# Cross attention: another order of scores, maxima and weighings on TensorE, and later batches' queries moved behind the lead

## The chip, the cores and the metric

One core of one Trainium2 chip runs the whole program. The metric is the device time of one execution in microseconds. Of the kernel before there are three timed runs.

## The reference, cut to what matters

The reference is a small Perceiver-like network: x has 4 batches of 256 tokens with 256 channels, and each of two layers has a cross attention to a context of 4 x 4096 tokens, a self attention and a feed-forward part. The change touches only the cross attention, which is stage 0 and stage 3 of six stages:

```
q = layernorm(x) @ Wq (+ bq);  k = ctx @ Wk (+ bk);  v = ctx @ Wv (+ bv)     # 16 heads of 16 channels
x = x + (softmax(q k^T / 4) v) @ Wo (+ bo)                                  # 256 queries, 4096 keys per batch
```

## The kernel before, in words

Class `Cross` holds one cross-attention stage. Each engine's method (`pe`, `act`, `dve`, `pool`, `sp`) walks the same list of steps, `self.plan`, and issues its own part of each step, so the order of the list in `steps` is the order of the instructions on every engine, SyncE's queue of DMAs among them.

The keys of a batch are worked in 4 blocks of 1024, so there are 16 items (batch, block). An item has 4 groups of 4 heads, and such a group is called a quad here: 64 quads in a stage. A quad has 8 slots, one for each 128 keys of its block. For each slot there are a `scores` step (L891, 4 matmuls of 256 columns on 50 rows in each half of the array, followed by ScalarE's exponential, L683, into one of `NE = 4` buffers) and a `weigh` step (L921, the exponentials times the values, accumulated in one PSUM bank, on 128 rows and 17 columns). Ahead of it, `LEAD = 18` slots early, there is a `max` step (L907, 2 matmuls of 512 columns on 48 rows, followed by VectorE's reduction, L759), which finds each query's maximum over the block. `scores` and `max` share three PSUM units in turn; a unit is free again once ScalarE or VectorE has read it (`before`). ScalarE may write the exponentials of slot n only once slot n - 4 has been weighed.

Other steps lie between these. After the eighth maximum of a quad `place_max` combines the maxima on VectorE (L770; for the last block of a batch also L774 and L780, whose result ScalarE exponentiates, L712) and splits them on GpSimd. `max_rows` turns them on TensorE (L936), and SyncE writes them into spare rows of the queries with 4 DMAs (L576), for which the first `scores` of the next quad waits (`m_in`). `gather` turns the sums of a finished quad (L929). `combine` has three parts on VectorE (L791, L794, and L800 on), in four quads for each batch. `turn_out` and `project_out` finish a batch.

The jobs are projections of the context: `key` (L863, 6 matmuls of 512 columns) and `value` (L877, 12 of 256), 4 of each for an item, and `query` (L853), two for a batch. Keys and queries are copied by ScalarE, split into two parts by GpSimd (L606, L608; the two buffers alternate, and `kp_out` makes GpSimd wait until the write of the last but one has landed), written to DRAM by SyncE (L538) and read back in another layout: a batch's queries by `stack_q` (12 DMAs, L548), after waiting until both writes have landed, and half an item's keys by `stack_k` (6 DMAs, L479). One `stack_k` is issued in each even quad.

In the order before, two slots make a pattern: score, maximum, two weighings, score, maximum, and then one side step, which is `max_rows` with `gather` at the beginning of a quad, and otherwise a job if one may run. Values of an item may run only after its buffer is free (`may_fill`), so that the 8 jobs of an item fall into the first three quads of four, and the fourth has none. The 18 maxima of the lead run ahead of any score, with two side steps after each pair of them; the queries of batches 1 to 3 are among these.

Of the kernel before, what the change touches and what calls it, by code (L numbers as in the profile page):

```python
# [14 lines left out]
B, S, D = 4, 256, 256  # L15
# [231 lines left out]
class Cross(Stage):  # L247
# [25 lines left out]
    LEAD = 18  # L273
# [67 lines left out]
    def filling(self):  # L341


        values = lambda i: [("value", i, t) for t in range(self.KT // 2)]
        queries = lambda b: [("query", b, mt) for mt in range(2)]
        first = values(0)
        out = self.keys(0, 1) + first[0:2] + queries(1) + first[2:4] + queries(2) + queries(3)
        for i in range(1, self.ITEMS):
            out += self.keys(i, 0) + self.keys(i, 1) + values(i)
        return out  # L350

    def steps(self):
# [5 lines left out]
        else:  # L358
# [4 lines left out]
        total = self.SLOTS * self.ITEMS  # L363
        batch = self.SLOTS * self.NKB
        jobs = self.filling()
        outputs = [(batch * (b + 1) + at, (kind, b)) for b in range(B)
                   for at, kind in ((18, "turn_out"), (22, "project_out"))]
        for t in range(-self.LEAD, total + 24, 2):
            top = t + self.LEAD
            quad, at = divmod(t, 8)  # L370
            side = []
            if at == 0 and 0 <= quad + 1 < 4 * self.ITEMS:
                side.append(("max_rows", quad + 1))
            if at == 0 and 0 <= quad - 2 < 4 * self.ITEMS:
                side.append(("gather", quad - 2))
            if not side and outputs and outputs[0][0] <= t:
                side.append(outputs.pop(0)[1])
            while len(side) < (2 if t < 0 else 1) and jobs and self.may_fill(jobs[0], t):
                side.append(jobs.pop(0))
            for odd in range(2):  # L380
                if 0 <= t + odd < total:
                    out.append(("scores", t + odd))
                if top < total:
                    out.append(("max", top + odd))
                if odd == 0:
                    out += [("weigh", n) for n in (t - 2, t - 1) if 0 <= n < total]
            if top < total and top % 8 == 6:
                out.append(("place_max", top // 8))
            for step in side:
                out.append(step)  # L390
# [702 lines left out]
class Conv(Stage):  # L1093
# [3 lines left out]
    G = H // GH  # L1097
# [2042 lines left out]
```

## Time and profile before

| | us |
|---|---|
| median of three runs | 4365.25 (4364.61 to 4373.9) |
| span of the profiled execution | 4357.8 |
| TensorE, matmuls, busy | 3998.4 (92% of the span) |
| VectorE busy | 3011.4 (69%) |
| ScalarE busy | 2806.9 (64%) |
| GpSimd busy | 1811.5 (42%) |

The profile gives no whole time of its own execution beside the span; the median of the runs is 7.45 us above the span. The first cross attention lies from 0 to about 985 us, the second from about 2908 to 3885 us. In the digits of the page (40 slices, busy share in tenths) TensorE is at 9 in nearly every slice of both stages:

```profile
PE   4999999988979999999999999967999999976998
DVE  4777777767777767767677676644787877767745
PEclk7999999999989999999999999988999999988999
```

### The profile page before, as it was taken

What the parts mean: (1) busy time and instruction counts of PE and PEld (TensorE: products, weight loads), DVE (VectorE), ACT (ScalarE), POOL (GpSimd) and SP (SyncE); (2) the same over time, 40 slices, a digit from 0 to 9 for tenths busy, and PEclk for the clock granted to TensorE, in tenths of its full rate; (3) what the DMA queues carried; (4) which work ended last, traced back from release to release, by engine and by line L of the source; (5) the groups of instructions that cost most, each with busy time, mean ns of one, the idle gap of its engine ahead of it and who ended that gap; (6) DMA issues with size and microseconds to landing.
All of it is one profiled execution on the core that took longest, in us unless ns stands there. A gap on an engine that the chain in (4) does not pass through costs nothing. (4 is left out here: it accounts for less than half of the span.)

```text
span 4357.8 us, 81373 instructions
## 1 busy us (share of the span) xinstructions
PE 3998.4 (92%) x30320; PEld 2853.4 (65%) x30320; DVE 3011.4 (69%) x6897; ACT 2806.9 (64%) x5769; POOL 1811.5 (42%) x1862
## 2 busy tenths in 40 slices
PE   4999999988979999999999999967999999976998
PEld 3555555545757787887888888854555555535777
DVE  4777777767777767767677676644787877767745
ACT  2777777677967767777676776723676767654322
POOL 3333333204556555555556555523322322202644
PEclk7999999999989999999999999988999999988999
DMA  6666665536020110010100101027666666512265
GB/s 167 119 118 118 115 110 114 103 50 217 1 78 5 35 35 28 25 37 26 37 25 25 37 25 39 13 54 154 115 114 113 115 113 112 99 27 72 85 191 186
DMA packets 208194, 354.02 MB, mean 81 GB/s; under 512 B 26927, under 2 KB 110564, under 8 KB 205745
## 3 DMA queue, kind: packets, MB, share of 16 engines
q1 hardware_dynamic: 200217, 338.42, 35.4%
q0 software_dynamic: 7584, 10.39, 0.7%
q8 instruction: 243, 3.98, 0.4%
q14 instruction: 150, 1.23, 0.1%
HBM read 257.48 MB, written 114.98 MB: 85 GB/s over the span
## 5 line engine op out<-in xcount | busy, mean ns | idle before, releaser
L759 DVE TENSOR_REDUCE xa_m_part<-xa_unit 128x2 f32<-128x1024 f32 x1024 | 1247.7, 1224 | 515.3 <-PE xa_unit L907 513.8
L683 ACT ACTIVATE xa_ex<-xa_unit 128x1024 f32<-128x1024 f32 x1024 | 1029.8, 1019 | 259.7 <-PE xa_unit L891 254.4
L921 PE MATMUL xa_pv<-xa_ex,xa_vs 128*17 128x256 f32 x8192 | 546.5, 383 | 7.1 <-ACT xa_ex L683 7.0
L907 PE MATMUL xa_unit<-xa_ks,xa_q_base 48*128 48x512 f32 x2048 | 437.9, 425 | 117.8 <-ACT xa_ex L683 85.8
L1068 POOL TENSOR_SCALAR lt_p<-lt_p,lt_stat 128x192 f32<-128x192 f32 x384 | 355.3, 926 | 453.6 <-DVE lt_stat L1058 453.0
L891 PEld LDWEIGHTS xa_unit<-xa_q_base,xa_ks 50*128 50x128 f32 x4096 | 312.1, 185 | 316.2 <-issue 242.5
L891 PE MATMUL xa_unit<-xa_q_base,xa_ks 50*128 50x256 f32 x4096 | 502.5, 324 | 10.2 <-DVE xa_m_part L759 6.1
L1911 PE MATMUL lt_bank<-lt_wp,lt_xt 128*128 128x512 f32 x1728 | 465.1, 411 | 14.3 <-DVE lt_wp L1748 6.3
L1078 ACT ACTIVATE lt_p<-lt_p,lt_stat 128x128 f32<-128x128 f32 (+1 forms) x768 | 321.7, 420 | 157.2 <-DVE lt_stat L1053 154.5
L1911 PEld LDWEIGHTS lt_bank<-lt_wp,lt_xt 128*128 128x128 f32 x1728 | 314.5, 192 | 78.8 <-DVE lt_xt L1741 9.1
L618 POOL TENSOR_SCALAR xa_m_neg<-xa_m_blk 128x8 f32<-128x8 f32 x128 | 29.9, 233 | 780.4 <-DVE xa_m_blk L770 780.4
L1625 POOL TENSOR_TENSOR lt_r_qk<-lt_r_qk,lt_t_rot 128x512 f32<-128x512 f32 x192 | 268.0, 1397 | 202.5 <-DVE lt_t_rot L1779 196.8
L1053 DVE CUSTOM_DVE_ANT_0 lt_p<-lt_bank,lt_mask,lt_rq 128x128 f32<-128x128 f32 (+1 forms) x768 | 261.3, 377 | 122.2 <-PE lt_bank L1017 119.2
L921 PEld LDWEIGHTS xa_pv<-xa_ex,xa_vs 128*17 128x17 f32 x8192 | 186.4, 96 | 238.9 <-issue 123.5
L907 PEld LDWEIGHTS xa_unit<-xa_ks,xa_q_base 48*128 48x128 f32 x2048 | 193.1, 186 | 170.0 <-ACT xa_ex L683 117.1
L1632 POOL TENSOR_TENSOR lt_nrm<-lt_nrm,minus_half 128x16 f32<-128x16 f32 x96 | 282.0, 2937 | 22.4 <-DVE lt_nrm L1796 19.7
L1998 PE MATMUL lt_bank<-lt_ft,lt_w 128*128 128x256 f32 x1152 | 267.4, 382 | 9.4 <-DVE lt_ft L1856 5.9
L1686 ACT ACTIVATE lt_t_sq<-lt_bank 128x512 f32<-128x512 f32 x192 | 114.9, 598 | 226.1 <-DVE lt_t_rot L1779 226.1
L1998 PEld LDWEIGHTS lt_bank<-lt_ft,lt_w 128*128 128x128 f32 x1152 | 214.5, 191 | 41.5 <-issue 12.7
L606 POOL CAST xa_kp<-xa_k 128x512 fp32r<-128x512 f32 (+1 forms) x144 | 86.4, 600 | 341.1 <-ACT xa_k L663 138.9
L863 PE MATMUL xa_side<-xa_cxp,xa_wp 128*128 128x512 f32 x720 | 203.4, 419 | 10.6 <-DVE xa_cxp L742 10.6
L877 PE MATMUL xa_side<-xa_wp,xa_cxp 128*128 128x256 f32 x1488 | 208.4, 290 | 0.0
(334 smaller groups left out, 7903.3 us busy)
## 6 DMA issues: line engine op xcount, KB each, us to landing
xa_ks<-keys SPq DMA_DIRECT2D x372, 256.0 KB
keys<-xa_kp SPq DMA_DIRECT2D x128, 512.0 KB, 3.3
xa_cx<-in_ctx_t SPq DMA_DIRECT2D x64, 512.0 KB
lt_u<-in_lt_wqkv SPq DMA_DIRECT2D x54, 256.0 KB
places<-in_moe_blank SPq DMA_DIRECT2D x47, 258.0 KB, 8.6
moe_xs<-places SPq DMA_DIRECT2D x47, 258.0 KB
lt_w<-in_lt_w SPq DMA_DIRECT2D x6, 1536.0 KB
xa_q_base<-xa_m_rows SPq DMA_DIRECT2D x512, 2.0 KB
```

Of the source, the lines that this page charges most:

```text
L683: act.activation(x.ex[:, n % x.NE, :, :], x.place_of[step][:, :, :].rearrange("p o (j s) -> p (o j) s", j=2), ACT.Exp).then_inc(*x.ex_done ...
L759: dve.tensor_reduce(x.m_part[:, i % 2, qt, 2 * pair:2 * pair + 2, ch:ch + 1], x.place_of[step][:, :, :], AX.X, ALU.max).then_inc(*x.dve_ou ...
L891: mm = pe.matmul(bank[:, odd, pair * S:pair * S + S], x.ks[unit % x.NU][rows, 2 * (g % 2) + pair, kt * P:(kt + 1) * P], x.q_base[rows, 2 * ...
L907: mm = pe.matmul(bank[:, odd, :], x.q_base[rows, pair, b * S + qt * P:b * S + (qt + 1) * P], x.ks[unit % x.NU][rows, pair % 4, ch * 512:(c ...
L921: mm = pe.matmul(x.pv[32 * j:32 * j + x.VW, 0:S], x.vs[:, i % x.NV, kt, 4 * g + j, :], x.ex[:, n % x.NE, 2 * (j % 2) + j // 2, :], start=( ...
L1053: dve.tensor_tensor_reduce(self.p[:, n % 5, to], s[:, at], st.mask[:, at], st.minus_scale(b, h, q), -NEG, ALU.add, ALU.min, t3[:, 0, q:q + ...
L1068: pool.tensor_scalar(sv, sv, self.stat[:, n % 5, 3, 1:2], None, ALU.mult).then_inc(*self.div_pool.one())
L1078: act.activation(low, low, ACT.Exp, bias=t3[:, 0, q:q + 1], scale=-1.0, accum_out=t3[:, 2, q:q + 1]).then_inc(*self.exp_done.one())
L1625: pool.tensor_tensor(out, out, self.t_rot[:, t, :], ALU.add).then_inc(*self.rot_add.one())
L1632: pool.tensor_tensor(n[:, 2, :], n[:, 1, :], c.minus_half[:, 0:H], ALU.pow).then_inc(*self.rnorm.one())
L1911: mm = pe.matmul(bank[:, :], self.xt[:, par, xpart, k, tile * P:(tile + 1) * P], self.wp[:, wpart, sec, k, half * 512:half * 512 + 512], s ...
L1998: mm = pe.matmul(bank[:, gate * S:(gate + 1) * S], self.w1[:, k, gate * FFP + m * P:gate * FFP + (m + 1) * P], self.ft[:, k, :], start=(k ...
```

## The change

`steps` is written anew. A quad is now one string of tokens, `ORDER`, gone through once for each quad: M a maximum, S a score, W a weighing, J a job, G the quad's `max_rows`, `gather` and (in even quads) `stack_k`, X an extra step, C a part of `combine`. The weighings are two slots behind the beginning of the quad (`BEHIND`), in runs of 2, 2 and 4. There are two jobs in each quad. The first item's remaining keys and all its values come ahead of the first maximum; in the lead there are only the second item's four `key` jobs, after the maxima 9, 12, 15 and 18. The queries of batch b + 1 are extra steps of quads 16b + 5 and 16b + 7, `turn_out` and `project_out` of quads 16b + 18 and 16b + 19. The second `query` step of a batch is followed at once by its `stack_q`.

```
--- before.py
+++ after.py
@@ -270,7 +270,9 @@
     NV = 2
     UNITS = 3
     NE = 4
-    LEAD = 18
+    LEAD, ROWS_AT = 18, 11
+    AHEAD = (9, 12, 15, 18)
+    ORDER, BEHIND = ("M S M W W X S M G S M C W W S M S J M C S M J S S M C W W W W").split(), 2
 
     def __init__(self, c, name, ctx_t, wq, wk, wv, wo, bq, bk, bv, bo, kscratch, load=None):
         super().__init__(c)
@@ -340,13 +342,21 @@
 
     def filling(self):
 
-
         values = lambda i: [("value", i, t) for t in range(self.KT // 2)]
-        queries = lambda b: [("query", b, mt) for mt in range(2)]
-        first = values(0)
-        out = self.keys(0, 1) + first[0:2] + queries(1) + first[2:4] + queries(2) + queries(3)
+        out = []
         for i in range(1, self.ITEMS):
             out += self.keys(i, 0) + self.keys(i, 1) + values(i)
+        return out
+
+    def follow(self, step):
+
+        out = [step]
+        if step[0] == "value" and step[2] % 2 == 1:
+            m = 2 * (step[1] + 1) + step[2] // 2
+            out += [("split", m)] if m < 2 * self.ITEMS else []
+            out += [("ctx", m + 2)] if m + 2 < 2 * self.ITEMS else []
+        if step[0] == "query" and step[2] == 1:
+            out.append(("stack_q", step[1]))
         return out
 
     def steps(self):
@@ -360,50 +370,64 @@
             out += keys[0:1] + [("split", 1), ("norm",)] + keys[1:2]
             out += queries[0:1] + [("stack_k", 0)] + queries[1:] + [("stack_q", 0), ("rest_k",)]
         out += [("ctx", 2), ("ctx", 3), ("late",)]
-        total = self.SLOTS * self.ITEMS
-        batch = self.SLOTS * self.NKB
+        for step in self.keys(0, 1) + [("value", 0, t) for t in range(self.KT // 2)]:
+            out += self.follow(step)
+            if step == ("key", 0, 1, 1):
+                out.append(("stack_k", 1))
+        total, quads = self.SLOTS * self.ITEMS, 4 * self.ITEMS
+        per_batch = 4 * self.NKB
         jobs = self.filling()
-        outputs = [(batch * (b + 1) + at, (kind, b)) for b in range(B)
-                   for at, kind in ((18, "turn_out"), (22, "project_out"))]
-        for t in range(-self.LEAD, total + 24, 2):
-            top = t + self.LEAD
-            quad, at = divmod(t, 8)
-            side = []
-            if at == 0 and 0 <= quad + 1 < 4 * self.ITEMS:
-                side.append(("max_rows", quad + 1))
-            if at == 0 and 0 <= quad - 2 < 4 * self.ITEMS:
-                side.append(("gather", quad - 2))
-            if not side and outputs and outputs[0][0] <= t:
-                side.append(outputs.pop(0)[1])
-            while len(side) < (2 if t < 0 else 1) and jobs and self.may_fill(jobs[0], t):
-                side.append(jobs.pop(0))
-            for odd in range(2):
-                if 0 <= t + odd < total:
-                    out.append(("scores", t + odd))
-                if top < total:
-                    out.append(("max", top + odd))
-                if odd == 0:
-                    out += [("weigh", n) for n in (t - 2, t - 1) if 0 <= n < total]
-            if top < total and top % 8 == 6:
-                out.append(("place_max", top // 8))
-            for step in side:
-                out.append(step)
-                if step[0] == "value" and step[2] % 2 == 1:
-                    m = 2 * (step[1] + 1) + step[2] // 2
-                    out += [("split", m)] if m < 2 * self.ITEMS else []
-                    out += [("ctx", m + 2)] if m + 2 < 2 * self.ITEMS else []
-                if step[0] == "query" and step[2] == 1:
-                    out.append(("stack_q", step[1]))
-            unit, at_u = divmod(t + 32, 16)
-            if at_u == 0 and 2 <= unit < 2 * self.ITEMS:
-                out.append(("stack_k", unit))
-            if t == 2 - self.LEAD:
-                out.append(("stack_k", 1))
-            if quad >= 2 and at >= 2:
-                b, kb = divmod((quad - 2) // 4, self.NKB)
-                if kb == self.NKB - 1 and b < B:
-                    out.append(("combine", b, (quad - 2) % 4, at // 2 - 1))
-        assert not jobs and not outputs
+        extra = {}
+        for b in range(B):
+            extra[per_batch * (b + 1) + 2], extra[per_batch * (b + 1) + 3] = ("turn_out", b), ("project_out", b)
+            if b + 1 < B:
+                extra[per_batch * b + 5], extra[per_batch * b + 7] = ("query", b + 1, 0), ("query", b + 1, 1)
+        top = 0
+
+        def maximum():
+            steps = [("max", top)]
+            return steps + [("place_max", top // 8)] if top % 8 == 7 else steps
+
+        while top < self.LEAD:
+            out += maximum()
+            top += 1
+            if top == self.ROWS_AT:
+                out.append(("max_rows", 0))
+            if top in self.AHEAD:
+                out += self.follow(jobs.pop(0))
+        for quad in range(quads + 4):
+            scores, weighs, parts = 8 * quad, 8 * quad - self.BEHIND, 0
+            b, kb = divmod((quad - 2) // 4, self.NKB)
+            summing = quad >= 2 and kb == self.NKB - 1 and b < B
+            for token in self.ORDER:
+                if token == "M" and top < total:
+                    out += maximum()
+                    top += 1
+                elif token == "S":
+                    if scores < total:
+                        out.append(("scores", scores))
+                    scores += 1
+                elif token == "W":
+                    if 0 <= weighs < total:
+                        out.append(("weigh", weighs))
+                    weighs += 1
+                elif token == "G":
+                    if quad + 1 < quads:
+                        out.append(("max_rows", quad + 1))
+                    if 0 <= quad - 2 < quads:
+                        out.append(("gather", quad - 2))
+                    if quad % 2 == 0 and quad // 2 + 2 < 2 * self.ITEMS:
+                        unit = quad // 2 + 2
+                        assert all(k in out for k in self.keys(unit // 2, unit % 2))
+                        out.append(("stack_k", unit))
+                elif token == "J" and jobs and self.may_fill(jobs[0], scores):
+                    out += self.follow(jobs.pop(0))
+                elif token == "X" and quad in extra:
+                    out += self.follow(extra.pop(quad))
+                elif token == "C" and summing:
+                    out.append(("combine", b, (quad - 2) % 4, parts))
+                    parts += 1
+        assert not jobs and not extra and top == total
         return out
 
     def may_fill(self, job, t):
```

## Rows read from the trace of the kernel before

Times in microseconds from the beginning of the span. "x4" is the number of instructions merged in a row; in brackets stands the idle time before it and what ended it.

**Rows 1.** TensorE in order of time, first stage: where quads begin (start, length, engine, line, operation).

```profile
101.14 0.59 PE L936 MATMUL xa_side<-ident,xa_m_cols 128*8 128x128 f32 x2
...
652.02 0.38 PE L936 MATMUL xa_side<-ident,xa_m_cols 128*8 128x128 f32 x2
...
664.18 0.38 PE L936 MATMUL xa_side<-ident,xa_m_cols 128*8 128x128 f32 x2
...
965.27 0.38 PE L936 MATMUL xa_side<-ident,xa_m_cols 128*8 128x128 f32 x2
```

**Rows 2.** TensorE in order of time within a quad that has jobs.

```profile
502.21 1.68 PE L877 MATMUL xa_side<-xa_wp,xa_cxp 128*128 128x256 f32 x12
503.82 0.50 PE L891 MATMUL xa_unit<-xa_q_base,xa_ks 50*128 50x256 f32 x4
504.16 0.39 PE L907 MATMUL xa_unit<-xa_ks,xa_q_base 48*128 48x512 f32 x2
504.48 1.06 PE L921 MATMUL xa_pv<-xa_ex,xa_vs 128*17 128x256 f32 x16
505.47 0.50 PE L891 MATMUL xa_unit<-xa_q_base,xa_ks 50*128 50x256 f32 x4
```

**Rows 3.** All engines in order of time in a quad without jobs.

```profile
652.55 0.50 PE L891 MATMUL xa_unit<-xa_q_base,xa_ks 50*128 50x256 f32 x4
...
657.78 0.40 PE L907 MATMUL xa_unit<-xa_ks,xa_q_base 48*128 48x512 f32 x2
657.99 1.94 ACT L683 ACTIVATE xa_ex<-xa_unit 128x1024 f32<-128x1024 f32 x2 [1.10 <-PE xa_unit L891]
658.01 0.41 PE L891 MATMUL xa_unit<-xa_q_base,xa_ks 50*128 50x256 f32 x4
658.23 1.23 DVE L759 TENSOR_REDUCE xa_m_part<-xa_unit 128x2 f32<-128x1024 f32 x1 [0.43 <-PE xa_unit L907]
659.06 0.49 PE L907 MATMUL xa_unit<-xa_ks,xa_q_base 48*128 48x512 f32 x2 [0.65 <-ACT xa_ex L683]
...
662.53 1.06 PE L921 MATMUL xa_pv<-xa_ex,xa_vs 128*17 128x256 f32 x16
...
663.66 0.39 ACT L693 ACTIVATE xa_o_sb<-xa_pv 128x256 f32<-128x256 f32 x1 [0.70 <-PE xa_pv L921]
```

**Rows 4.** VectorE's combining and ScalarE's exponential of the block weights, in order of time.

```profile
504.26 0.23 ACT L712 ACTIVATE xa_w_blk<-xa_w_blk 128x32 f32<-128x32 f32 x1 [1.14 <-DVE xa_w_blk L780]
...
533.83 1.14 DVE L794 TENSOR_REDUCE xa_acc<-xa_o_all 128x136 f32<-128x544 f32 x1
```

**Rows 5.** SyncE's queue in the lead of the first stage, in order of time.

```profile
57.24 2.67 SPq L479 DMA_DIRECT2D xa_ks<-keys  x6
59.95 0.94 SPq L538 DMA_DIRECT2D keys<-xa_kp  x2
71.92 5.47 SPq L548 DMA_DIRECT2D xa_q_base<-keys  x12
...
89.30 2.42 SPq L576 DMA_DIRECT2D xa_q_base<-xa_m_rows  x4
```

**Rows 6.** TensorE in the same lead: waits for queries' copies, then the first scores.

```profile
73.18 2.93 PE L863 MATMUL xa_pv<-xa_cxp,xa_wp 128*128 128x512 f32 x6 [10.78 <-ACT xa_k L660]
...
92.83 0.50 PE L891 MATMUL xa_unit<-xa_q_base,xa_ks 50*128 50x256 f32 x4 [2.19 <-issue]
...
100.42 0.80 PE L907 MATMUL xa_unit<-xa_ks,xa_q_base 48*128 48x512 f32 x2 [6.61 <-ACT xa_ex L683]
```

**Rows 7.** SyncE's queue within quad 6 of the first stage.

```profile
191.75 2.68 SPq L479 DMA_DIRECT2D xa_ks<-keys  x6
195.53 4.28 SPq L538 DMA_DIRECT2D keys<-xa_kp  x2
```

**Rows 8.** DMA issues, us to landing: the write begun at 195.53, then all 144 such writes.

```profile
keys<-xa_kp SPq DMA_DIRECT2D x1, 512.0 KB, 12.6
...
DMA to landing us min/median/max: 2.1/3.3/13.6
```

## The prediction

> **What bounds the kernel now.** I read the page's busy shares, then TensorE in order of time, then the other engines in the same stretches, then SyncE's queue.
>
> From the first quad's beginning to that of quad 62 a stage takes 965.27 - 101.14 = 864.1 us, 62 quads of 13.94 in the mean. The last quad of an item, which has no jobs, takes 664.18 - 652.02 = 12.16, so the three others some 14.5 each [rows 1]. The reader is to see that in a quad with jobs TensorE's blocks simply follow one another: a value job 1.61, a score 0.34, a maximum 0.32, two weighings 0.99 [rows 2]. In a quad without jobs there are holes: the maximum at 659.06 waits 0.65 for an exponential, since two scores met with one maximum between them and three PSUM units [rows 3]. TensorE's order sets the time of quads with jobs, the round through ScalarE that of the others. Before quad 0 lies another kind of loss: waits of 10.78, 2.19 and 6.61 for copies, rows and exponentials, all held up by the queries of batches 1 to 3 [rows 6].
>
> **The blocks' prices.** A maximum followed by a score costs 658.01 - 657.78 = 0.23, followed by a weighing 0.32; a score after other work costs 0.34, and takes the same matmul columns as a maximum [rows 2, 3]. So I read: 0.23 for each score or maximum inside a run, 0.11 at the run's entry (its first weights are not loaded ahead), 0.10 at its exit. Two scores in a row are nowhere in these rows; between 0.23 (as maximum and score) and 0.34 (as at an entry) I take 0.23, whose columns they have. Two weighings are 0.99, of which I read 2 x 0.43 and 0.12 for the switch; a run of four is then 1.85. `max_rows` with `gather` takes 652.55 - 652.02 = 0.53 [rows 1, 3].
>
> **A plain quad of the new order.** It has 6 runs of scores and maxima (3, 2, 2, 3, 3, 3; before it had 7 to 8), 3 of weighings (before 4), 2 jobs. 16 x 0.23 + 6 x 0.21 + 8 x 0.43 + 3 x 0.12 + 0.53 + 2 x 1.6 = 12.5. The same sum for a quad of the order before with three jobs is 14.7; the rows give 14.5 for the mean of quads with three, three and two.
>
> To this the waits are added, walked through one quad. An exponential takes 1.02, two in a row 1.94, and begins 0.55 after its score's begin; VectorE begins 0.45 after a maximum and takes 1.23 [rows 3]. A weighing is known to be done 0.27 after its last columns: 662.53 + 0.86 + 0.27 = 663.66 [rows 3]. In the new order scores 6 and 7 stand before the four weighings 2 to 5. With `NE = 4` the exponential of score 6 needs weighing 2, that of score 7 weighing 3. So it begins 0.7 after the run of four begins, the next ends at 0.7 + 0.92 + 1.02 = 2.65; but TensorE is through the run and the next maximum at 1.85 + 0.34 = 2.2, and the next quad's first score needs the PSUM unit of score 7. Wait: 0.5, and 0.1 for weights no longer loaded ahead. With two small waits of 0.1 and their loads a plain quad is 13.4. That is a new wait, and it eats over half of what the order saves against the mean of 13.94. The same walk gives 14.8, 14.75, 13.9 and 12.1 for the four quads of an item before, 13.89 in the mean against 13.94, so I trust it to 0.2.
>
> Two kinds of quads cost more. In 16 quads of a stage, the last blocks' maxima, ScalarE stands 1.14 at L712 behind VectorE [rows 4]; there the exponential of score 5 is queued behind it, score 7 needs its unit, and waits 0.75. In 12 quads with `combine`, the 1.14 of L794 [rows 4] comes between the sixth and seventh maximum, and the eighth, which needs the seventh's unit, waits 1.1; before, a side step lay over it. Four quads without jobs are 12.5, bound by the same waits. Together: 58 x 13.4 + 4 x 12.5 + 16 x 0.75 + 12 x 1.1 = 852.4. The six query steps (0.97 each) now stand in this stretch, and `turn_out` and `project_out` (2.5 a batch, as before): 865.7. The walk of the order before gives 859.2 where 864.1 is seen; with the same 4.9 the new stretch is 870. **Term: +6 a stage, +12**, between -18 and +40 (0.2 a quad either way).
>
> **The lead.** Gone are the six query jobs with three times 12 DMAs. Their chain is what TensorE waited for: `stack_k` of unit 1 is issued at 57.24, the queries' writes behind it at 59.95, and they have landed when `stack_q` goes out at 71.92 [rows 5]; only then are buffers free, and it goes on so with batches 2 and 3. What is late next is `stack_k` of unit 1 itself, needed by maximum 16. It can hardly start before 56, since its keys' writes wait in the same queue as now. Its reads take some 14 us, as the 14.7 from 57.24 to 71.92 show: 70. Behind it two context loads and one key write, 1.5 MB, an estimated 4 us, stand before the rows of `max_rows`, with 2.42 for their issue and 1.1 until the score at 92.83 [rows 5, 6]; the scores start at 75, and quad 0 at 77 instead of 101.14 [rows 1]. The second `stack_k` comes 2 late. Gain 22 to 24; the second stage has the same steps, and I take the same. **Term: -24 a stage, -48**, between -20 and -66. The first item's jobs, moved ahead of the maxima, run while TensorE waits for its first queries.
>
> **The queries' new place.** Quads 7, 23 and 39 hold the second query step, and behind it on SyncE stand `stack_q` (wait for landing, 12 issues) and then `max_rows`, without which the next quad's first score can't start. Times from quad 7's `max_rows` on TensorE: GpSimd may split the query only once the write of the last but one chunk has landed. That is quad 6's first key job, and quad 6 is even, so a `stack_k` lies ahead of it. The row shows just this case: `stack_k` issued at 191.75, a key write at 195.53, landed 12.6 later, against 3.3 in the median [rows 7, 8]. In the new quad 6 the first job ends 4.9 after `max_rows` by the prices above; copy and split, an estimated 2.6, bring its write to 7.5, 3.8 behind the `stack_k` as in the rows, so it lands at 20.1. Quad 6 takes 14.3 (it ends with the query step), which makes it 5.8. Then the split until 7.0 (1.2, an estimate), half of a pair of issues 0.5 [rows 5], the median landing 3.3: 10.8; `stack_q`'s issues 5.47: 16.3; the rows' 2.42 and 1.1: 19.7. The score is due at 11.1 (a quad of 13.4, less 2.3 between its first score and `max_rows`). Wait: 8.6 us, and TensorE can't go round it. After the wait of 6.61 the maximum took 0.80 instead of 0.39 [rows 2, 6]: that is TensorE at the lower of its two levels (1.2 and 2.4 GHz) after standing idle. If the first maximum, weighings' switch, score, maximum and `max_rows` after a wait cost twice, that is 0.32 + 0.12 + 0.34 + 0.32 + 0.53 = 1.6 more; I take 1.7. **Term: 6 x 10.3 = +62**, between +15 (below) and +90.
>
> Here a rule of the Trainium skill speaks against the change: "DMA: Bandwidth & Descriptors", in the section on queues, rings and completion order, has a DMA's semaphore increment land only after every earlier write of that DMA engine. By that rule the 12.6 is the write's place in the queue and comes back each time: +62; without it one would count with the median: +17. This trace's 12.6 agrees with it.
>
> **The end.** Quads 62 and 63 have `combine` and no jobs: 0.85 more each; the last exponential waits for its buffer, 0.8. **+2.5 a stage, +5.**
>
> **Sum** against the profiled execution: -48 + 12 + 62 + 5 = +31, span 4389. The median is 7.45 above the span, so I forecast 4396.
>
> **Rivals.** *The stacking is quick* (other side). If quad 6's write lands in the median 3.3 [rows 8], GpSimd splits at once, `stack_q` goes out at 4.9, the rows land at 13.9, and the wait is 2.9 without a fall of the clock: 17 instead of 62, time 4351, faster. It decides at the landing: with `max_rows` landed before 11.1 the wait is nothing. For it: the median of 144 writes; against: the row with a `stack_k` ahead. *The quads are cheaper than walked*: if the exponentials of scores 6 and 7 slip in before the first score needs the unit, 0.35 less in 116 quads, -40: 4356, about no change. Against it is the calculation from `NE = 4`; for it, that ScalarE is busy only 1.94 of the 3.0 between two such waits [rows 3]. *Everything in the queue is later*: rows of quad 0 behind more traffic, lead gain 12 a stage, waits of 12: 4440. *The change does not do what it says*: the runs of three leave as much waiting as they take away. That is already so in the walk (+6 a stage), and lies within the forecast.
>
> **Chances.** Forecast 0.58, quick stacking 0.16, cheaper quads 0.14, later queue 0.12. The forecast's own range is 4370 to 4425. 0.2% (8.7 us) is about what a measurement of this kernel can tell from no change. Faster: all of the quick stacking and a part of the cheap quads, 0.21; within: 0.10; slower: 0.69. Range 4335 to 4430.
>
> **What would show it.** TensorE waits of 8 to 9 us, by DMA, at L891 at the start of quads 8, 24 and 40 of each stage; the clock below full after them. Quad 0 at 77 (not below 68, not above 90). Plain quads of 13.4, those after a `combine` 14.4, with a wait of 0.5 on L683 at the first score. If plain quads are at 12.8 or the three waits below 4, the prediction is wrong, and the change is faster.

## The result and the profile after

The changed kernel takes 4459.08 us in the median (4455.69 to 4470.25, 4 runs) against 4367.53 of the kernel before on the same chip (4364.61 to 4373.9, 4 runs): ratio 1.0207, 95% interval 1.0194 to 1.0219. The direction was forecast, the size was not: 4396 was the forecast, and its range ended at 4430.

The first stage counted from the beginning of the span, the second from its layer norm, each up to the layer norm behind it, both together take 2077.2 us instead of 1986.7, +90.5; the layers between them take 1911.9 instead of 1911.4. So the whole difference of the medians (91.5) lies in these two stages. By their parts, as the prediction cut them:

| term, both stages | forecast | measured |
| --- | --- | --- |
| lead, up to quad 0 | -48 | -21.6 - 23.5 = -45.1 |
| quad 0 to quad 62, stalls included | +12 + 62 = +74 | +71.0 + 64.9 = +135.9 |
| behind quad 62 | +5 | -0.8 + 0.7 = -0.1 |

TensorE in order of time in the changed kernel, first stage: where quads 0, 2, 3, 5, 6, 7 and 8 begin, and the beginning of quad 62 (start, length, engine, line, operation). It answers to [rows 1].

```profile
79.53 0.38 PE L960 MATMUL xa_side<-ident,xa_m_cols 128*8 128x128 f32 x2
...
108.10 0.38 PE L960 MATMUL xa_side<-ident,xa_m_cols 128*8 128x128 f32 x2
...
122.51 0.38 PE L960 MATMUL xa_side<-ident,xa_m_cols 128*8 128x128 f32 x2
...
151.51 0.38 PE L960 MATMUL xa_side<-ident,xa_m_cols 128*8 128x128 f32 x2
...
165.01 0.38 PE L960 MATMUL xa_side<-ident,xa_m_cols 128*8 128x128 f32 x2
...
180.52 0.38 PE L960 MATMUL xa_side<-ident,xa_m_cols 128*8 128x128 f32 x2
...
201.60 0.59 PE L960 MATMUL xa_side<-ident,xa_m_cols 128*8 128x128 f32 x2
...
1014.62 0.38 PE L960 MATMUL xa_side<-ident,xa_m_cols 128*8 128x128 f32 x2
```

The reader sees three kinds of quads; a key quad is one whose two jobs are `key` jobs, a value quad one with `value` jobs. Quad 5, with value jobs, takes 165.01 - 151.51 = 13.50, as forecast (13.4). Quad 7 takes 201.60 - 180.52 = 21.08: the stall. Quad 2, with key jobs and nothing else, takes 122.51 - 108.10 = 14.41, a full 1.0 more than forecast, and that is new. 24 of the 28 key quads of the first stage cost so much too much, or more.

Quad 2 in three engines shows why. VectorE, GpSimd and TensorE of the changed kernel (in brackets the idle time before, and what ended it):

```profile
113.52 1.22 DVE L783 TENSOR_REDUCE xa_m_part<-xa_unit 128x2 f32<-128x1024 f32 x1 [1.03 <-PE xa_unit L931]
114.77 1.07 DVE L794 TENSOR_TENSOR xa_m_blk<-xa_m_part 128x8 f32<-128x8 f32 x1
115.76 1.21 DVE L783 TENSOR_REDUCE xa_m_part<-xa_unit 128x2 f32<-128x1024 f32 x1
```

```profile
113.83 0.61 POOL L630 CAST xa_kp<-xa_k 128x512 fp32r<-128x512 f32 x1 [8.37 <-ACT xa_k L679]
114.52 1.30 POOL L632 TENSOR_TENSOR xa_kp<-xa_k,xa_kp 128x512 fp32r<-128x512 f32 x1
```

```profile
115.44 0.74 PE L915 MATMUL xa_unit<-xa_q_base,xa_ks 50*128 50x256 f32 x8
117.03 0.50 PE L931 MATMUL xa_unit<-xa_ks,xa_q_base 48*128 48x512 f32 x2 [0.84 <-DVE xa_m_part L783]
...
120.20 0.50 PE L915 MATMUL xa_unit<-xa_q_base,xa_ks 50*128 50x256 f32 x4 [0.40 <-ACT xa_ex L707]
```

L794, the first step of `place_max`, is the maximum of two small tiles of 8 elements a partition. It begins 0.25 after GpSimd's subtraction for the low part of a key and ends with it (114.77 + 1.07 = 115.84; 114.52 + 1.30 = 115.82). The same line over the whole kernel, min/median/max in ns, after and before:

```profile
L794 DVE TENSOR_TENSOR xa_m_blk<-xa_m_part x128: 166/167/2357, 52.0 to 3952.9; 128x8 f32<-128x8 f32 x128
```

```profile
L770 DVE TENSOR_TENSOR xa_m_blk<-xa_m_part x128: 166/168/170, 54.6 to 3863.4; 128x8 f32<-128x8 f32 x128
```

Laid against GpSimd's rows of the whole kernel, 51 of the 128 begin during such a subtraction (0.07 to 0.34 us into it); all 51 take 0.97 to 1.24 and end 0.02 to 0.03 behind it. Two more, the longest, stand in the leads: they begin 0.03 us into GpSimd's longer subtraction for the context (L622), take 2.36 and 2.34, and end with it. One begins within a copy of GpSimd's and takes 0.46. The other 74 take 0.17.

In the kernel before, none of the 128 met a key's subtraction, and the 28 that begin within the one for the context do so in its last 0.04 us. But a hold was there to be seen, at another VectorE instruction with two inputs in SBUF, `combine`'s L804: six of its 32 took 0.60 or 0.61 instead of 0.29. VectorE, then GpSimd of the kernel before:

```profile
338.85 0.61 DVE L804 TENSOR_TENSOR xa_att<-xa_acc,xa_rec 128x128 f32<-128x128 f32 x1
```

```profile
336.92 2.39 POOL L598 TENSOR_TENSOR xa_cxp<-xa_cx,xa_cxp 128x1024 fp32r<-128x1024 f32 x1
```

Back in the changed kernel: behind L794 in VectorE's queue stands the reduction that frees the PSUM unit, so TensorE's next maximum waits 0.84. Of the 28 key quads of the first stage 24 have such a hold (the others are 7, 23, 39 and 55; in 23 it is the one of 0.46), and no value quad has one. The 0.40 at 120.20 is the wait for `NE = 4` that was forecast as 0.5.

In the 16 quads of the last blocks, two more rows of VectorE follow L794 and ScalarE waits for them at L736 before it goes on with the exponentials. ScalarE, then TensorE of the changed kernel in such a quad; it answers to [rows 4]:

```profile
487.44 0.23 ACT L736 ACTIVATE xa_w_blk<-xa_w_blk 128x32 f32<-128x32 f32 x1 [2.58 <-DVE xa_w_blk L804]
```

```profile
488.63 0.50 PE L915 MATMUL xa_unit<-xa_q_base,xa_ks 50*128 50x256 f32 x4 [1.58 <-ACT xa_ex L707]
...
489.30 3.37 PE L945 MATMUL xa_pv<-xa_ex,xa_vs 128*17 128x256 f32 x32
```

The wait is 2.58 where it was 1.14, the score waits 1.58 instead of the 0.75 I had walked, and the four weighings behind it take 3.37 instead of the 1.92 of undisturbed quads: TensorE's granted clock, at its full level before (2.4 GHz), was 0.65 on average from 488.6 to 493.5. Such key quads of a last block (10 and 11, 16.1 each), and the key quads with a `combine` (14 and 15, 16.4 and 16.3), cost the most. The first stage has twelve of the two kinds, each with one wait of 1.57 to 1.85: in eight of them the granted clock of the quad was 0.89 to 0.90, and they take 16.1 to 16.4; in four (27, 30, 43 and 46) it stayed at 1.00, and they take 15.1 to 15.4.

The stall at quad 8, TensorE and then SyncE's queue. It answers to [rows 7, 8] and to the forecast wait of 8.6:

```profile
197.46 0.79 PE L915 MATMUL xa_unit<-xa_q_base,xa_ks 50*128 50x256 f32 x4 [6.14 <-DMA xa_q_base<-xa_m_rows]
198.02 0.66 PE L931 MATMUL xa_unit<-xa_ks,xa_q_base 48*128 48x512 f32 x2
198.61 1.91 PE L945 MATMUL xa_pv<-xa_ex,xa_vs 128*17 128x256 f32 x16
```

```profile
185.95 0.36 SPq L562 DMA_DIRECT2D keys<-xa_kp  x1
188.06 5.76 SPq L572 DMA_DIRECT2D xa_q_base<-keys  x12
193.87 2.41 SPq L600 DMA_DIRECT2D xa_q_base<-xa_m_rows  x4
```

Busy time and granted clock of the stretch from quad 0 to quad 62 (window; its length, PE, PEld, DVE, ACT, POOL busy; clock, DMA share, GB/s), after and then before:

```profile
79.50:1014.60 935.10, 846.10 (x8294) 507.19 (x8294) 661.76 (x657) 616.04 (x821) 247.80 (x369) 0.96 0.56 104
```

```profile
101.10:965.30 864.20, 823.27 (x8275) 481.91 (x8274) 650.89 (x657) 608.21 (x815) 246.91 (x359) 1.00 0.60 109
```

Of the 71 us that the stretch grew, 846.1 - 823.3 = 22.8 are TensorE's busy time, for 19 matmuls more; the rest is waiting. The clock was 1.00 and is 0.96. So long waits can be paid twice, once as they stand and once in the lower clock behind them. The short ones are not: quads 2 and 3, with waits of 0.84 and 0.40, are at 1.00 throughout.

### The profile page after: what moved, and what is told of

The parts are those of the page before. It is cut to its first block and busy times, and to the rows that moved or that the text cites. A ratio compares the mean times of both kernels' runs of the same rounds, so it can differ in the third digit from the quotient of the medians.

```text
span 4459.2 us, 81371 instructions
## 1 busy us (share of the span) xinstructions
PE 4038.2 (91%) x30320; PEld 2901.4 (65%) x30320; DVE 3037.0 (68%) x6897; ACT 2816.4 (63%) x5769; POOL 1804.6 (40%) x1862
## 3 DMA queue, kind: packets, MB, share of 16 engines
q14 instruction: 150, 1.23, 0.1%
## 5 line engine op out<-in xcount | busy, mean ns | idle before, releaser
L783 DVE TENSOR_REDUCE xa_m_part<-xa_unit 128x2 f32<-128x1024 f32 x1024 | 1235.9, 1221 | 571.7 <-PE xa_unit L931 570.8
L707 ACT ACTIVATE xa_ex<-xa_unit 128x1024 f32<-128x1024 f32 x1024 | 1017.3, 1020 | 441.0 <-PE xa_unit L915 230.5
L915 PE MATMUL xa_unit<-xa_q_base,xa_ks 50*128 50x256 f32 x4096 | 473.2, 317 | 118.0 <-ACT xa_ex L707 76.0
L931 PE MATMUL xa_unit<-xa_ks,xa_q_base 48*128 48x512 f32 x2048 | 469.0, 457 | 105.9 <-DVE xa_m_part L783 57.4
L945 PE MATMUL xa_pv<-xa_ex,xa_vs 128*17 128x256 f32 x8192 | 557.8, 404 | 0.7 <-ACT xa_ex L707 0.7
L915 PEld LDWEIGHTS xa_unit<-xa_q_base,xa_ks 50*128 50x128 f32 x4096 | 327.9, 190 | 334.4 <-issue 166.4
L945 PEld LDWEIGHTS xa_pv<-xa_ex,xa_vs 128*17 128x17 f32 x8192 | 209.4, 101 | 244.8 <-issue 126.7
L2022 PEld LDWEIGHTS lt_bank<-lt_ft,lt_w 128*128 128x128 f32 x1152 | 214.6, 191 | 41.7 <-issue 12.6
```

What stands on the lines that cost most here:

```text
L707: act.activation(x.ex[:, n % x.NE, :, :], x.place_of[step][:, :, :].rearrange("p o (j s) -> p (o j) s", j=2), ACT.Exp).then_inc(*x.ex_done ...
L783: dve.tensor_reduce(x.m_part[:, i % 2, qt, 2 * pair:2 * pair + 2, ch:ch + 1], x.place_of[step][:, :, :], AX.X, ALU.max).then_inc(*x.dve_ou ...
L915: mm = pe.matmul(bank[:, odd, pair * S:pair * S + S], x.ks[unit % x.NU][rows, 2 * (g % 2) + pair, kt * P:(kt + 1) * P], x.q_base[rows, 2 * ...
L931: mm = pe.matmul(bank[:, odd, :], x.q_base[rows, pair, b * S + qt * P:b * S + (qt + 1) * P], x.ks[unit % x.NU][rows, pair % 4, ch * 512:(c ...
L945: mm = pe.matmul(x.pv[32 * j:32 * j + x.VW, 0:S], x.vs[:, i % x.NV, kt, 4 * g + j, :], x.ex[:, n % x.NE, 2 * (j % 2) + j // 2, :], start=( ...
L2022: mm = pe.matmul(bank[:, gate * S:(gate + 1) * S], self.w1[:, k, gate * FFP + m * P:gate * FFP + (m + 1) * P], self.ft[:, k, :], start=(k ...
```

## Experiments

Ratios are to the kernel before on the same chip (4338 to 4340 us on some chips, 4368 to 4370 on others), so kernels are compared by ratio, or by the length of the two stages together: 1986.7 before, 2077.2 after. In the profiles the chips differ behind these stages: from the last layer norm on, 351 to 353 us on the former, 376 to 387 on the latter. Each number of one stage is from the profiled execution.

**One input instead of two.**

```
-  dve.tensor_tensor(m_blk[:, kb, :, :], x.m_part[:, i % 2, :, hs, 0], x.m_part[:, i % 2, :, hs, 1], ALU.max)
+  dve.tensor_reduce(m_blk[:, kb, :, :]..., x.m_part[:, i % 2, :, hs, :], AX.X, ALU.max)
```

> The changed kernel, but the maximum of the two half maxima (L794, a tensor_tensor of two inputs that both lie in SBUF) is a tensor_reduce over the same numbers, which reads one input. Theory A (while GpSimd's tensor_tensor of a key's low part runs, VectorE's instruction with two SBUF inputs stands still): in the changed kernel 54 of 128 such instructions took longer than 0.2 us, 48 us in all, and ended when GpSimd's did; with one input none is longer than 0.3, a plain key quad falls from 14.41 to about 13.5, about 25 us a stage at most, and the time is 4400 to 4420; the subtraction L804 in last-block quads still has two SBUF inputs and may keep a part. Theory B (the key quads cost more for another reason: their write and stack transfers, or ScalarE's copies out of the units): the line's duration or at least the quads stay as they are, 4459 within 5.

Measured: 1.0106 (1.0089 to 1.0122), stages 2032.4, 44.8 less than the changed kernel. The line, in this kernel:

```profile
L794 DVE TENSOR_REDUCE xa_m_blk<-xa_m_part x128: 170/170/172, 51.0 to 3909.4; 128x8 f32<-128x16 f32 x128
```

None is longer than 0.17, though 45 of the 128 begin within GpSimd's subtraction for a key, and quad 2 takes 13.51 instead of 14.41. Set side by side quad by quad in the first stage, each of the 24 with a hold is shorter by 0.44 to 1.81, and the value quads away from the stalls are the same within 0.06 from quad 4 on. Theory A stands: one instruction of 8 elements, issued a moment too early, cost half of what the change lost. TensorE's busy time from quad 0 to 62 fell by 10.8 (835.3) and its idle time by 11.3: about half of the gain is busy time, and the clock was 0.97 instead of 0.96. The expectation's last clause came true as well: the other instruction with two inputs in SBUF, the subtraction L804 of the last blocks, is now held in 11 of 32 cases (0.53 to 0.64 instead of 0.19); in the changed kernel none was.

**What holds it: two inputs on GpSimd, or GpSimd at all?** This kernel leaves out the true low parts of the keys, so its results are wrong.

```
-  pool.tensor_tensor(low, whole, high.bitcast(F32), ALU.subtract)
+  pool.tensor_copy(low, whole)
```

> The changed kernel, but GpSimd's key low part is a copy of the key (one input, 0.61 us as the copy ahead of it) instead of the subtraction of two (1.28); the low parts it writes are not those of the reference. Theory A1 (any GpSimd instruction that works in SBUF holds VectorE's two-input one back until its end): L794 in the key quads takes about 0.45 (it begins some 0.25 after GpSimd's) instead of 1.07, the sum falls from 70 to about 40 us and the key quads lose 0.6 or more: 1.012 to 1.016 of before. Theory A2 (only a GpSimd instruction with two inputs does): every L794 takes 0.17, the sum is 22 us, as with one input, and the time 1.0106 as there.

Measured: 1.0107 (1.0090 to 1.0123). VectorE, then GpSimd in quad 2 of this kernel:

```profile
115.79 0.37 DVE L794 TENSOR_TENSOR xa_m_blk<-xa_m_part 128x8 f32<-128x8 f32 x1
```

```profile
115.53 0.62 POOL L632 CAST xa_kp<-xa_k 128x512 fp32r<-128x512 f32 x1
```

Again it ends with GpSimd's, 116.16 and 116.15, though that reads one input. 45 begin within the second copy (0.27 to 0.50, median 0.37); the line's sum is 31.4 us, between 69.6 and 21.8. So A1 is right about the hold and too high about its length, and the time is that of A2: a hold of 0.2 costs 0.2 (quad 2 took 13.71), and the clock of quads 10, 11, 14 and 15 stays at 1.00. The Trainium skill, "SBUF — State Buffer", in its section on the two separate sides, has this as a lock: VectorE with two inputs in SBUF and a GpSimd instruction that reads SBUF share a port pair, and the one that starts second "fully blocks". These runs agree (1.07 behind 1.30, 0.37 behind 0.62, 0.17 with one input).

**The stacking of the queries two quads later.**

```
-        if step[0] == "query" and step[2] == 1:
-            out.append(("stack_q", step[1]))
...
+                    if quad % per_batch == 9 and quad // per_batch + 1 < B:
+                        out.append(("stack_q", quad // per_batch + 1))
```

> The changed kernel, but stack_q stands two quads later, behind max_rows of the quad in which the rows of quad 8 (of 24, of 40) have gone out, so that no max_rows waits behind it in SyncE's queue. If the three waits of up to 7.2 us and the lower clock after them come from the place of stack_q in that queue, they go: quads 7, 23, 39 fall by about 7.7 and the next by about 2, six times: 57 us less, 4402. Rival: the landing of the queries' write, which is late behind a stack_k, holds up the queue whatever stands behind it (GpSimd's splits of the next keys wait for the same buffers): then the wait appears at another place, and less than half is won, above 4430.

Measured: 1.0095 (1.0078 to 1.0112), stages 2024.9, 52.3 less. TensorE's waits in the quads of the first stage by what ended them (us in total, times, longest), in the changed kernel and in this one:

```profile
PE xa_unit L915 <- ACT xa_ex L707: 35.9, 62, 1.6
PE xa_unit L931 <- DVE xa_m_part L783: 27.0, 25, 1.8
PE xa_unit L915 <- DMA xa_q_base<-xa_m_rows: 19.4, 3, 7.2
```

```profile
PE xa_unit L915 <- ACT xa_ex L707: 36.7, 64, 1.7
PE xa_unit L931 <- DVE xa_m_part L783: 28.1, 26, 1.8
...
PE xa_unit L931 <- DMA xa_ks<-keys: 0.4, 1, 0.4
```

The three waits of up to 7.2 us are gone and nothing took their place; quads 7 and 8 take 13.54 and 13.51 instead of 21.08 and 15.39, and the key quads' waits for VectorE are as they were.

**Both.** The two edits above (the first and the third) in one kernel.

> The two edits that each took about 1% from the changed kernel, together: the half maxima's maximum with one SBUF input, and stack_q two quads later. If what they remove is independent (VectorE standing behind GpSimd in the key quads; the queue of SyncE in three quads a stage), the gains add up: 45.7 - 90.5 + 38.2 - 90.5 = 97 us off the changed kernel's two stages, so 0.9985 of the kernel before (0.9965 to 1.0005). If they share waits (the queue's stalls lie in key quads), less is won: 1.004 or more.

Measured: 0.9976 (0.9966 to 0.9985), stages 1974.2, 103.0 less. The gains add up (44.8 + 52.3 = 97.1). The change with these two faults mended is a little faster than the kernel before, not 2% slower. The hold is not all gone: L804 is held in all twelve key quads of the last blocks. VectorE, then GpSimd of this kernel:

```profile
224.86 0.63 DVE L804 TENSOR_TENSOR xa_w_blk<-xa_m_blk,xa_m_all 128x32 f32<-128x32 f32 x1
```

```profile
224.16 1.29 POOL L632 TENSOR_TENSOR xa_kp<-xa_k,xa_kp 128x512 fp32r<-128x512 f32 x1
```

Such a key quad takes 14.76 in the mean of the first stage, a value quad of the same blocks, whose L804 takes 0.19, 14.29.

**The two halves of the change by themselves.** The new order with the queries left in the lead (cut: more places for jobs in the lead, and no query steps in the quads):

```
-        out = []
+        out = [("query", b, mt) for b in range(1, B) for mt in range(2)]
```

> The changed kernel with its new order of the slots, but the queries of batches 1 to 3 back in the lead as before. Expected: lead +22 a stage (+45), the three stalls a stage gone (-57), the six query steps out of the stretch of quads but in the lead: 4459 + 45 - 57 = 4447, within 8. If the new order of the slots is what costs (key quads +30 a stage against what I worked out), this kernel is about 80 slower than the one before (4367). Rival (the order is harmless and all of the loss hangs on the queries' place): 4380 or less.

and the old order with the queries moved into empty job places:

```
             out += self.keys(i, 0) + self.keys(i, 1)
+            if i % self.NKB == 2 and i // self.NKB + 1 < B:
+                out += queries(i // self.NKB + 1)
             out += values(i)
```

> The kernel before with the order of its quads untouched; only the queries of batches 1 to 3 leave the lead and go, a batch at a time, into job places of items 2, 6 and 10 that were empty. If the lead's gain does not need the new order of the slots, quad 0 begins at about 78 instead of 101.14 and the stage's lead gives 22; stack_q is again ahead of some max_rows, so each of three places a stage costs up to 10: from 4322 (all hidden) to 4375 (all as in the changed kernel). Rival (the queries cost the same wherever they stand): 4365 within 9.

Measured: the order alone 1.0197 (1.0180 to 1.0214), stages +84.2 against before; the queries alone 0.9958 (0.9944 to 0.9971), stages -17.4. So the loss is the order's. The queries' lead gives 16.2 and 16.4 a stage here, not 22: quad 0 begins at 85.0, not 79.5; I did not take apart how much of that is the first item's jobs, which only the changed kernel puts ahead of the maxima. Its quads lose 9.0 and 6.3 again, and one wait, for keys whose `stack_k` stands in SyncE's queue behind the queries, is of the kind of the stalls above (TensorE of this kernel):

```profile
395.80 0.79 PE L909 MATMUL xa_unit<-xa_ks,xa_q_base 48*128 48x512 f32 x2 [3.22 <-DMA xa_ks<-keys]
```

**Late stacking in the old order** (in quads 9, 25 and 41).

> The order of before, the queries in job places of items 2, 6 and 10, and stack_q in quads 9, 25 and 41 behind their max_rows. The kernel that differs from it only in the place of stack_q took 0.9958 of before and showed in its first stage one wait of 3.2 us for stacked keys and a quad of 21.2 instead of 14.8. If they come from stack_q in SyncE's queue, 6 to 9 us a stage go: 0.992 to 0.993. If not, 0.996.

Measured: 0.9931 (0.9914 to 0.9947), stages 1954.3. The wait is gone, and the quads are back at 865.7 and 865.3, with the six query steps in them.

**A fifth buffer for the exponentials**, `NE = 5`, with the one input and the late stacking:

> The same, with five buffers for the exponentials instead of four. My walk of the new order puts a wait of 0.5 in each of 116 plain quads (with what it costs in weights not loaded ahead) down to the four buffers: the exponential of score 6 can't begin before weighing 2 is done, and the next quad's first score waits for its unit. With five, both go an entire weighing earlier: plain quads of 13.0 instead of 13.5, 50 us less than the kernel without it, 0.987 of the kernel before. Rival: the wait is PSUM's (three units) or ScalarE's own pace, and the fifth buffer moves it by nothing: 0.9985.

Measured: 0.9824 (0.9807 to 0.9841), 62 us less than with four. TensorE's waits for exponentials in the first stage, with four buffers and with five:

```profile
PE xa_unit L915 <- ACT xa_ex L707: 36.9, 71, 1.4
```

```profile
PE xa_unit L915 <- ACT xa_ex L707: 14.9, 16, 1.5
```

The wait that the new order brought with it was the four buffers', as walked in the prediction; taking it away gave 62 where 50 was expected.

**place_max one maximum later**, with its two inputs, and the late stacking; four buffers:

```
-            return steps + [("place_max", top // 8)] if top % 8 == 7 else steps
+            return steps + [("place_max", top // 8 - 1)] if top % 8 == 0 and top else steps
```

> The changed kernel with stack_q two quads later, and place_max one maximum later in the plan, still with its instruction of two SBUF inputs. Theory A (it stands still only while GpSimd's tensor_tensor of the same moment runs): moved by some 2 us it mostly no longer meets it, its sum falls from 68 us to 30 or less, and the time from 1.0095 of before to 1.000 or less; in the last blocks' quads ScalarE's wait for VectorE also moves behind an exponential, which could give 0.75 in 32 quads more. Theory B (two SBUF inputs are slow whatever GpSimd does, in this order): the sum stays at 68 us and the time at 1.0095. A danger: max_rows of that quad comes later by the same 2 us, which could make the first score of a quad wait for its rows.

Measured: 0.9886 (0.9869 to 0.9902), stages 1936.0. The line in this kernel:

```profile
L796 DVE TENSOR_TENSOR xa_m_blk<-xa_m_part x128: 136/156/1326, 52.8 to 3812.2; 128x8 f32<-128x8 f32 x128
```

Theory A again, by time instead of by input: its sum is 26.6, not 68. 22 still begin within a key's subtraction, but 17 of them in its last 0.14 us, with next to nothing left to wait for; the five that begin earlier take 0.49 to 1.20. This edit gives 89 where the one input gave 51 (late stacking in both). The waits for an exponential fell to 22.8 us in 58 (36.9 in 71 with one input), none over 0.4. In the last blocks ScalarE now has an exponential done before it waits for VectorE: quads 10 to 13 take 13.34 each, no more than plain ones, where with one input they took 14.71, 14.73, 14.30 and 14.31. The danger, rows that come too late, did not come about. What did come, and was not foreseen, is the hold at `combine`'s instructions with two inputs. GpSimd, then VectorE, then TensorE in quad 17 of this kernel:

```profile
323.58 2.49 POOL L624 TENSOR_TENSOR xa_cxp<-xa_cx,xa_cxp 128x1024 fp32r<-128x1024 f32 x1
```

```profile
323.94 2.68 DVE L837 TENSOR_TENSOR xa_att<-xa_att,xa_bv 128x512 f32<-128x512 f32 x1
```

```profile
328.41 0.50 PE L917 MATMUL xa_unit<-xa_q_base,xa_ks 50*128 50x256 f32 x4 [1.02 <-DVE xa_m_part L785]
```

L837 took 0.69 in the kernel with one input and late stacking; quads 17, 33 and 49 of the first stage take 16.3 here where they took 15.3, 15.2 and 15.2. The kernel with five buffers below keeps this.

**All of it, and how many buffers.**

> The new order with stack_q two quads later, place_max one maximum later, and five buffers for the exponentials. With four buffers it took 0.9886 of before; the fifth took 62 us from the kernel that reads one input. If the wait that the fifth buffer removes is untouched by the place of place_max, 50 to 60 us go here too: 0.975 to 0.977 (4230 to 4238 where before is 4338). If the late place_max already took a part of that wait (57 waits of up to 0.4 instead of 69 of up to 1.4 for an exponential in the first stage), about 30: 0.982.

> As the kernel with five buffers, with six. By my walk a fifth buffer already lets the exponential of score 7 start before the first weighing of the run of four is done, so the sixth brings nothing: within 5 us of the kernel with five. Rival (the buffers still bind, since in the last blocks' quads ScalarE stands behind VectorE and its exponentials bunch up): 10 to 20 us more.

> The order of before, queries in empty job places, stack_q late, and five buffers. In the order of before the waits for an exponential lie in the quads without jobs (57 waits, 30 us in the first stage of the kernel with four). Theory A (they come from the four buffers there too): up to 25 a stage go, 0.982. Theory B (they come from two scores that meet with one maximum between them and three PSUM units, as I read the row of the wait of 0.65): nothing goes, 0.993. Set against the kernel with the new order and five buffers it gives what the order is worth once its own waits are gone.

Measured: the new order with late stacking, late place_max and five buffers 0.9799 (0.9786 to 0.9813), 4284.58 us where before takes 4370.06, the fastest kernel; stages 1904.6. That is 31 less than with four buffers, my second guess: the late `place_max` had taken a part of the buffers' wait. With six buffers 0.9820 (0.9805 to 0.9835), stages 1902.0: nothing more, as walked. The old order, its queries out of the lead and stacked late, with five buffers 0.9940 (0.9924 to 0.9955), the same as with four; its waits for exponentials, with four and with five, in the first stage:

```profile
PE xa_unit L909 <- ACT xa_ex L685: 30.3, 57, 0.7
```

```profile
PE xa_unit L909 <- ACT xa_ex L685: 30.5, 58, 0.7
```

So there they do not come from the four buffers; that they come from two scores that meet, as the row of 0.65 was read [rows 3], fits but was not tried. Set against each other with five buffers and the queries out of the lead, the order of the slots, with its late `place_max`, is worth 1958.1 - 1904.6 = 53.5 us: what it saves shows only once its own three waits are gone or smaller. The stretch of quads of the fastest kernel, columns as above:

```profile
77.70:926.30 848.60, 809.69 (x8297) 499.75 (x8296) 645.23 (x657) 615.59 (x821) 248.22 (x369) 0.99 0.62 114
```

## Why the prediction was right and wrong

- **The lead** (-48): right, -45.1. Quad 0 begins at 79.5 (forecast 77), and what is late before it is `stack_k` of unit 1, as said: TensorE waits 10.62 for its landing until 73.08.
- **The queries' stall** (+62): right in place, cause and nearly in size. The late landing did come back (quad 6's first key write, issued at 172.77, landed 11.8 later; forecast 12.6), and `stack_q` in the queue held `max_rows`: from quad 7's `max_rows` it was through at 193.82 - 180.52 = 13.3, where 16.3 was forecast, and the score began at 16.9 instead of 19.7. The three waits of the first stage are 19.4 in all, 6.5 each, not 8.6; quad 8 behind took 15.39 instead of 13.50, 1.9 for the clock, forecast 1.7. Taking it away gave 52 (58 where the hold was gone already).
- **The plain quad of 13.4**: right for value quads (13.50), with its wait for `NE = 4`, which experiments with five and six buffers bear out.
- **The quads' term** (+12, between -18 and +40): the step that failed. In it key quads were priced as value quads, and VectorE's step after the eighth maximum with its 0.17 of before. I walked TensorE, ScalarE and VectorE, and GpSimd not at all. The new order puts a quad's two key jobs so that GpSimd's subtraction runs just when `place_max` starts, and L794 takes about 1.07 instead of 0.17; in the order before not one of 128 had met one. The one input took away 44.8 of it (51 with late stacking).
- **What is left**: with both faults mended the quads of a stage take 882.0 and 880.9, together 33.8 more than before where +12 was forecast. These 22 are what else the walk had wrong, 11 a stage. Quads 58 to 60, without jobs, take 14.3, 15.6 and 14.4 where 12.5 + 0.75 was forecast, 4.5 together (each has a wait of 1.34 or 1.35, and a granted clock of 0.78 to 0.88); the six key quads of the last blocks 14.8 in the mean where 13.4 + 0.75 was, 3.7 together. Of these 3.7 some 2.9 are GpSimd's hold again, on L804 (14.76 against 14.29 in value quads, six times), so the walk without GpSimd cost more than the 40 below. The rest is 0.1 to 0.2 in many quads. The late `place_max` takes the first two away (13.2, 13.3 and 13.4; five of the six 13.3 to 13.4), so quads 58 to 60, which have no hold, hung on the order of VectorE's and ScalarE's steps about it.
- So the miss, 135.9 - 74 = 62, is: stall and hold together 135.9 - 33.8 = 102, of which 62 was forecast, makes 40; and 22 from the rest of the walk.
- **The end** (+5): -0.1. The last exponentials' wait for a buffer did not reach the end of the stage.
- **The rivals.** Quick stacking: no. Cheaper quads: no. Later queue: its time (4440) was nearest, its mechanism did not show. None had GpSimd in it.

## What to carry to other kernels

When instructions are reordered, walk every engine, the idle one too: an engine at 40% can hold another's instruction for as long as its own takes. A short combining step of two SBUF tiles on VectorE is best written with one input, or put behind the reduction that frees a buffer; both helped here, and each left or made a hold at the next instruction with two inputs, so all of them are to be walked. And an order that groups work needs its buffers counted again: here the same order is 2% slower or 2% faster than the old one, by one buffer, one step's place and one queue entry.

## What the runs showed of the hardware that was not expected

- A VectorE instruction of 8 elements a partition with two SBUF inputs takes 0.17 us alone, 0.97 to 1.24 when it begins 0.07 to 0.34 into a GpSimd subtraction of 1.30 (51 of 51), and 0.37 in the median within a GpSimd copy of 0.62 (0.27 to 0.50 in all 45 within the second copy). It ends with GpSimd's; begun in the last 0.04 us of it, it takes what it takes alone (28 in the kernel before). With one input it takes 0.17 in all 128. One of 128x512 elements took 2.68 instead of 0.69 (L837, with late `place_max`).
- The reductions L783, which have one input and read PSUM, are not held: all 1024 of the changed kernel take 1.19 to 1.23, those beside GpSimd's casts and subtractions too.
- A wait of 1.6 us can cost clock: after one of 1.58 four weighings took 3.37 instead of 1.92, but of the twelve quads with a wait of 1.57 to 1.85 four stayed at full clock, and what decides between them was not found. After a wait of 6.14 the granted clock was 0.50 from 197.4 to 206; in quads 9, 12, 13 and 16 to 22, with waits of up to 0.96, it stayed at 1.00; in quads 58 to 60, which have no jobs, it was 0.78 to 0.88, with waits of up to 1.35. With most waits gone, TensorE's busy time for as many matmuls (8294 and 8297 records) fell from 846 to 810 us in the first stage.
